# First attention with one small PE unit a step, engines' parts set apart, and experts begun from six batches

## The reference, cut to what matters

```python
x = x + attn0(layernorm(x))     # differential attention
x = x + ffn0(layernorm(x))      # 8 experts, 2 of them per token, capacity 1280 rows
x = x + attn1(layernorm(x))     # causal attention, 16 heads of 64
x = x + ffn1(layernorm(x))      # 8 experts, 4 per token, and a shared one

def attn0(x):                   # 16 heads of 8
    q, k, v = heads(x @ Wq.T + bq), heads(x @ Wk.T + bk), heads(x @ Wv.T + bv)
    x1 = softmax(q[:, :8] @ k[:, :8].T * 8 ** -0.5) @ v[:, :8]
    x2 = softmax(q[:, 8:] @ k[:, 8:].T * 8 ** -0.5) @ v[:, 8:]
    return concatenate([x1 - lv * x2, x2]) @ Wp.T + bp

def ffn0(x):
    probs, selected = top_k(softmax(x @ router.T), 2)       # probs divided by their sum
    # of each expert's tokens the 1280 with the largest weight are kept, ties in order of token
    # kept rows are dispatched to their expert's list, the rest is dropped
    out = (pre(rows) * silu(gate(rows))) @ post             # 128 -> 512 -> 128
    return sum of a token's kept outputs by its kept weights, divided by their sum
```

## Time and profile before

| | us |
|---|---|
| median of 3 runs | 1673.18 (1672.67 to 1674.95) |
| profiled execution | 1670.91 |
| its span on the core | 1667.8 |
| PE busy | 1540.4 |
| DVE busy | 1119.1 |
| ACT busy | 962.3 |
| POOL busy | 749.1 |

### The profile page before, as it was taken

How to read it: one execution, slowest core, us unless ns; L and a number is a source line. 1 busy time by engine, 2 the same in 40 slices (tenths; PEclk the granted TensorE clock), 3 DMA queues, 4 the chain that set the end, 5 groups by cost and what they waited for, 6 DMA issues and landing times.

```text
span 1667.8 us, 27765 instructions
## 1 busy us (share of the span) xinstructions
PE 1540.4 (92%) x9447; PEld 939.3 (56%) x9447; DVE 1119.1 (67%) x3559; ACT 962.3 (58%) x2484; POOL 749.1 (45%) x1237
## 2 busy tenths in 40 slices
PE   3779999998898999998899999999999999999998
PEld 2324334433334878897456565555656565657776
DVE  5669999899883567654666767767676767673322
ACT  2467767677675323333566767667675757674333
POOL 6122543453336665546453545545363634342221
PEclk9989999999999999999999999999999999999999
DMA  5447634663514565567000000000000000000000
GB/s 127 125 67 133 122 110 74 124 137 104 87 41 157 162 206 173 177 208 239 21 14 1 11 4 8 8 4 11 1 14 1 14 1 1 1 1 1 20 14 20
DMA packets 65984, 114.52 MB, mean 69 GB/s; under 512 B 13114, under 2 KB 32444, under 8 KB 65836
## 3 DMA queue, kind: packets, MB, share of 16 engines
q0 software_dynamic: 28608, 71.28, 19.3%
q1 hardware_dynamic: 36800, 40.69, 7.5%
q10 hardware_dynamic: 436, 0.79, 0.1%
HBM read 73.05 MB, written 39.78 MB: 68 GB/s over the span
## 4 chain that ended last, share of the span: by engine, by line
PE 53%; DVE 21%; ACT 11%; POOL 6%; issue 5%; DMA 4%; ACTq 0%; POOLq 0%; DVEq 0%
DVE mx L1565 7%; PE bank L1183 6%; ACT ar L1401 5%; PE pS L1150 5%; PE bank L1163 4%; PE bank L1192 4%; PE bank L992 3%; PE pS L962 3%; PE pS L1068 3%; PE pS L1069 3%; PE bank L1245 3%; PE bank L1120 3%; PE bank L1135 2%; PE bank L1083 2%; PE bank L1131 2%
## 5 line engine op out<-in xcount | busy, mean ns | idle before, releaser
L2130 POOL TENSOR_SCALAR ar<-ar,rd 128x512 f32<-128x512 f32 (+3 forms) x512 | 263.8, 535 | 305.4 <-DVE rd L1864 305.1
L1401 ACT ACTIVATE ar<-ar,nm 128x512 f32<-128x512 f32 (+3 forms) x512 | 284.9, 558 | 170.9 <-DVE nm L1855 170.7
L1565 DVE TENSOR_REDUCE mx<-pS 128x1 f32<-128x512 f32 x512 | 320.1, 680 | 54.2 <-PE pS L962 53.1
L1318 ACT ACTIVATE ar<-bank 128x512 f32<-128x512 f32 x342 | 193.9, 596 | 92.8 <-PE bank L983 92.0
L1855 DVE CUSTOM_DVE_ANT_0 ar<-pS,maskf 128x512 f32<-128x512 f32 (+3 forms) x512 | 228.2, 483 | 16.5 <-PE pS L1150 14.4
L962 PE MATMUL pS<-all_r 64*128 64x512 f32 x512 | 211.4, 493 | 27.0 <-DVE mx L1565 19.0
L1163 PE MATMUL bank<-identr,all_r 128*128 128x128 f32 x1280 | 201.0, 287 | 17.0 <-ACT ar L1411 9.5
L1163 PEld LDWEIGHTS bank<-identr,all_r 128*128 128x128 f32 x1280 | 133.0, 142 | 118.8 <-issue 81.9
L962 PEld LDWEIGHTS pS<-all_r 64*128 64x128 f32 x512 | 92.0, 198 | 174.3 <-DVE mx L1565 163.1
L1150 PE MATMUL pS<-ar 64*128 64x512 f32 (+3 forms) x1024 | 173.7, 458 | 0.0
L1357 ACT ACTIVATE ar<-pS 128x256 f32<-128x256 f32 (+1 forms) x200 | 70.3, 351 | 161.1 <-PE pS L1069 160.0
(11 more groups left out here) (251 smaller groups left out, 2858.7 us busy)
## 6 DMA issues: line engine op xcount, KB each, us to landing
rows_in<-zrow SPq DMA_DIRECT2D x16, 1024.0 KB, 4.6
all_r<-dk POOLq DMA_DIRECT2D x28, 256.0 KB, 8.4
dk<-xT SPq DMA_DIRECT2D x21, 256.0 KB, 4.4
rows_out<-ar SPq DMA_DIRECT2D x35, 128.0 KB, 4.0
dq<-xT SPq DMA_DIRECT2D x16, 256.0 KB, 2.9
all_r<-dq POOLq DMA_DIRECT2D x14, 288.0 KB, 6.6
all_r<-dq POOLq DMA_DIRECT2D x14, 256.0 KB, 4.8
x<-in_x SPq DMA_DIRECT2D x8, 256.0 KB, 3.8
```

The costliest lines, as they stand in the source:

```text
L1318: S.activation(pt[n % NPT], bST[n % 3], ACT.Exp, scale=QK_SCALE).then_inc(*s_ex.inc(Gr, kb, j))
L1401: S.activation(p, p, ACT.Exp, bias=nm1[:, c:c + 1], scale=-1.0, accum_out=den1[:, c:c + 1]).then_inc(*s_e1.inc(u, a))
L1565: V.tensor_reduce(mx[Gr % 2][:, col:col + 1], bS[n % 3], AX.X, ALU.max, negate=True).then_inc(*s_mx.inc(Gr, c))
L2130: G.tensor_scalar(p, p, rd1[:, c + a:c + a + 1], 1.0, ALU.mult, ALU.mult).then_inc(*s_p1.inc(u, a))
```

## The change

**The first attention's list.** Two functions take the generators' place. `beside(b, at)` names the one misc-bank unit of step `at` (0 to 15 within a batch), which now stands right behind the four pv and ahead of the fourth score unit. `behind(b, at)` names what the engines other than PE do at the end of the step, mostly two steps before it is used.

```diff
+    def beside(b, at):
+        Gr, p = 4 * b + at // 4, b - 1
+        if at % 4 == 0:
+            return [("shift", Gr + 1)] if Gr + 1 < NG else []
+        if at % 4 == 1:
+            return [("fin", Gr - 1)] if Gr else []
+        units = {2: ("at", p), 3: ("op", p), 6: ("v", b + 1), 7: ("turn", b + 2), 10: ("rturn", p),
+                 11: ("logits", "r", p), 14: ("q", b + 2), 15: ("k", b + 2)}
+        if b == NB - 1 and at == 6:
+            return [("table", 0)]
...
+    def behind(b, at):
+        Gr, p, n = 4 * b + at // 4, b - 1, b + 2
+        if at % 4 == 1 and Gr + 1 < NG:
+            add("land", Gr + 1)
+        if at % 4 == 3 and Gr + 2 < NG:
+            add("parts", Gr + 2)
...
                 if n == 3:
-                    if 4 * g + kb in PREP_AT:
-                        next(work, None)
                     if before[0] >= 0:
-                        for i in JS:
+                        for i in order_of(before[0]):
                             add("pv", *before, i)
+                    if kb == 0 and Gr > 0:
+                        add("take", Gr - 1)
+                    for unit in beside(b, 4 * g + kb):
+                        add(*unit)
```

**Normalization on ACT.** For batches 2 to 7 before the attention and 0 to 6 before the router:

```diff
+        def scale(stage, b, half):
+            rstd, nm = ln_sets[LN_SET[stage]][3:5]
+            ACTE.wait_ge(*s_rstd.at(stage, b))
...
+            for t in (2 * half, 2 * half + 1):
+                ins = S.activation(dst[:, t, :], x[:, 4 * b + t, :], ACT.Identity, bias=nm[:, t:t + 1],
+                                   scale=rstd[:, t:t + 1])
```

**Shift.** One transposition of 128 x 32 in place of four of 128 x 8:

```diff
-            for q in range(4):
-                ins = M.transpose(misc[0:8, 128 * q:128 * q + 128], mp[i][:, q, :], identf[:, :])
-            ins.then_inc(*s_full.inc("shift", Gr))
+            M.transpose(misc[0:32, 0:128].bitcast(F32R), mp[i][:, :, :].rearrange("p q c -> p (q c)").bitcast(F32R),
+                        identr[:, :]).then_inc(*s_full.inc("shift", Gr))
...
-            S.copy(mT[i], misc[0:8, :]).then_inc(*s_mact.inc("shift", Gr))
+            S.copy(mT[i], misc[0:32, 0:128]).then_inc(*s_mact.inc("shift", Gr))
...
-    dm = [dram(f"dm{i}", [8, 512]) for i in range(2)]
+    dm = [dram(f"dm{i}", [32, 128]) for i in range(2)]
```

```diff
+    for n, more in enumerate(([("k", 1)], [("low", "k", 1)], [("v", 1), ("zero", 1)], [])):
+        for unit in quarter(0, n) + more:
             add(*unit)
     add("parts", 0)
     add("shift", 0)
     add("land", 0)
...
+            if Gr == 0 and kb == 1:
+                add("late", 0)
+            if Gr == 2 and kb == 1:
+                add("late", 1)
```

```diff
+EARLY = 6 * 4 - (E - 1)
+PARTS = ((0, 0, EARLY), (0, EARLY, NCH[0] - EARLY), (1, 0, NCH[1]))
...
-    side = chained(last_batch(), route(NB - 1), table(1), qk_weights(), capacity())
+    side = in_turn(chained(last_batch(), route(NB - 1), table(2), qk_weights(), capacity()),
+                   chained(list_rows(NB - 2), table(1)))
```

More of the change, by code:

```diff
@@ L168, in route, with list_rows, table @@
             yield
-    def table(h):
-        add("table", h)
+            yield
+    def list_rows(b):
+        add("place", b)
         yield
-    def lead():
-        for p in range(2):
-            add("weights", p)
-            add("rows", p)
-            yield
+        yield
+        add("rows_at", b)
+        yield
+        yield
+        for t in range(4):
+            add("scatter", b, t)
+            yield
+            yield
+    def table(part):
+        add("table", part)
+        yield
@@ new lines, in in_turn @@
+    def in_turn(*parts):
+        parts = list(parts)
+        while parts:
+            for p in list(parts):
+                if next(p, p) is p:
+                    parts.remove(p)
+                else:
+                    yield
+    def beside(b, at):
[8 more added lines that the diff above has]
+            return [("table", 0)]
+        u = units.get(at)
+        return [u] if u and 0 <= u[-1] < NB and u != ("v", 1) else []
@@ L180, in schedule @@
     add("zero", 0)
-    first, second, stacks = prep(0), prep(1), stack(0)
-    for part in (first, first, second, first, second, first, first, second):
-        next(part)
+    for unit in (("ln", "p", 0), ("ones_of_v",), ("apply", "p", 0), ("ln", "p", 1), ("turn", 0), ("apply", "p", 1),
+                 ("q", 0), ("low", "q", 0), ("k", 0), ("low", "k", 0), ("turn", 1)):
+        add(*unit)
     for m in range(8):
-        next(stacks)
-    next(first)
-    for x in second:
-        pass
-    add("lam")
@@ L201, in schedule, with order_of @@
     add("land", 0)
-    for kb in range(2):
-        for unit in quarter(1, kb):
-            add(*unit)
-    PREP_AT = (9, 11, 12, 13, 14, 1)
-    STACK_AT = (0, 1, 2, 2, 3, 3, 4, 5)
-    work, proj, rout = iter(()), iter(()), []
-    ready = False
-    def route_step():
-        while rout:
-            if next(rout[0], 0) != 0:
-                return
-            rout.pop(0)
+    for b in range(2):
+        add("bias_x", b)
+    add("ones", 1)
+    for n in range(4):
+        for unit in quarter(1, n):
+            add(*unit)
+    add("lam")
+    add("parts", 1)
+    def order_of(Gr):
+        return JS if Gr + 2 < NG else (0, 1, 2, 3)
     for Gr in range(NG):
@@ L1698, in table @@
             after()
[L1699 to L1700 removed]
+            V.scalar_tensor_tensor(tiles(ridx[h][:, per * first:per * (first + nch)]), each(t_e), float(LIST[h]), loc,
+                                   ALU.mult, ALU.add).then_inc(*s_tab.inc(part))
         def hidden(p, f):
```

398 lines of the change are left out of this document (228 added, 170 removed).

## The result

The changed kernel took 1688.66 us, median of four runs (1683.43 to 1689.90), against 1672.93 before: ratio 1.0091, 95% interval 1.0063 to 1.0118. Slower, where 28 us faster was forecast. Run again later on another chip it stood at 1.0020 (0.9990 to 1.0049).

The account below looks back on a forecast made before the run. A first-attention batch was taken as DVE's work plus 5.2 us of its idle time, with PE setting the pace in the last groups. Terms -11 - 7 - 7 - 5 - 1 + 3.3 = -27.7 gave 1645 us; range 1614 to 1676.

Parts of the forecast that it names:

- Part a: Prologue to group 0's take: earlier first scores and exp, fewer maxima left for later; -11 us, bounds -2 and -16.
- Part f: Experts: earlier rows and spread scatters save, table 1 and the flush block before pass 37 cost; +3.3 us, bounds -7 and +8.
- Part c: Batches 1 to 5: normalizations leave DVE, its idle time stays; 55.0 us a batch in place of 56.4, -7 us.
- Rival B: First attention: the unit behind pv adds its whole length to DVE's hole; +50 us, 1695 us; chance 0.14.
- Part b: Groups 1 to 3: split x loads free the landing's DMA queue; 39 us in place of 45.9, -7, bounds 0 and -9.
- Part d: Batch 6: less DVE work and waiting, 51.7 us in place of 56.4; -5 us, bounds 0 and -7.
- Part e: Batch 7: table 0 moves to step 6 into DVE's slack, place goes; -1 us, bounds +2 and -4.
- Rival C: Groups 0 and 1: the new wait for x[2] keeps PE at its lower clock; 1655 us; chance 0.12.

Follow-up runs that it names:

- second pair: The changed kernel and the kernel before, both unaltered, run and profiled again on another chip: ratio 1.0020 (0.9990 to 1.0049).
- e5: Changed kernel with all stacks drawn first at each step's end, ahead of land and parts: 0.9922 of the kernel before.
- e13: Changed kernel with only the small unit moved behind the step's last score and exp product, stacks still behind parts: 1.0001 of the kernel before.
- e6: Changed kernel with stacks first and the small unit behind the step's last score and exp product: 0.9799 of the kernel before.
- e9: Changed kernel with stacks first, unit last, table 0 at step 14 of batch 7, weights and rows 0 and 1 behind it: 0.9825 of the kernel before.
- e11: Changed kernel with stacks first, unit last, table 0 at step 8 of batch 7: 1648.30 us, 0.9859 of the kernel before; 0.9796 on another chip.
- e15: Changed kernel with stacks first, unit last, table 0 at step 8, last two groups' exp and pv in old order 0, 2, 1, 3: 0.9794 of the kernel before.
- e10: Changed kernel with stacks first, unit last, table 0 at step 14 of batch 7, shift in its old form: 0.9787 of the kernel before.
- e1: Changed kernel with only the eighth stack moved, to the end of step 4, ahead of land: 1675.47 us, 1.0036 of the kernel before.
- e3: Changed kernel with table 0 at step 7 of batch 7 in place of step 6: 1.0062 of the kernel before.
- e2: Changed kernel with the shift in its old form (four transpositions, 8 pieces of 2 KB), order untouched: 1678.07 us, 1.0036 of the kernel before.

## Why the prediction was wrong, by its steps

- **Part a was right in sum**: -10.9 against -11, take 0 at 78.03 against 78, and it is -11.3 in the second pair. Its terms were off both ways: the first scores start at 32.2 us (31 forecast) and the first exp at 60.2 (58.3 forecast, so 3.0 us won and not 4.9), while from there to take 0 it is 7.9 us less where 5.8 was forecast. The stretched normalization was read rightly: it takes 1.12 us now.
- **Part f** was right in sum in the first pair, +3.8 against +3.3, and in kind: 12.7 us at the flush are 9 more than the neighbours, and the first pass no longer waits for rows. That the sum fits is partly luck. From the last take to the first transposition it gave -1.6 (forecast -2.5), from there to the last outward product +2.9 (forecast +5.8), and behind that, where nothing was forecast, +2.4, which no run explains. In the second pair f is +11.3, +8.1 of it between the first transposition and the last outward product.
- **Part c is the step that failed.** The work was right (48.95 us of DVE against 48.9, ACT's normalization 0.48 us against 0.46, ACT's 42 us no bound). The idle time was not: I wrote 5.3 us and "0.7 for the k rows that land from DRAM"; it was 11 in batch 4 and 9.2 to 11.5 in batches 1 to 5. Two things are in it. First, POOL's queue: PE waits 14.0 us for dk in six batches, 2.3 a batch, and mending it won 2.2 us a batch alone (e5) and 3.1 with the unit moved (e13 to e6). I had listed what `behind` does and seen that stacks kept their steps, but not that inside a step they had changed places with parts. The shift's way I "cost at nothing, since the landing is used two steps on": true of the exp that it feeds, untrue of what stands behind land in POOL's queue.
- Second, "some 0.35 us more that its queued work does not cover" at five units a batch: the hole is 0.73 us behind q and 0.68 behind k, and only the unit's place makes it; with both orders mended the same units left 2.2 us of wait for scores in a whole batch. There a batch's idle time is 53.56 - 48.84 = 4.7 us, near my 5.3: the estimate fitted an order that the change did not have.
- **Rival B** named this mechanism, with its place, but priced it at the unit's whole length, 8.4 us a batch; the unit's place measured 2.2 (alone) to 3.1 us, 13 to 19 us in six batches. B alone would not have eaten the gain of 28. It took the queue, which was in no rival, and batch 7.
- **Part b** gave -2.3 of -7: group 1 still took 17.6 us. The split of the x loads did not free it; PE waited there 1.3 us for the landing and 2.6 us for dk.
- **Part d** gave +0.2 of -5: DVE's idle time was 9.7 us in place of 6.0, by the same two causes, and its work 47.0 in place of 45.8. With both orders mended batch 6 takes 51.7 us (e6), the length forecast.
- **Part e**: +9.3 against -1. I wrote that table 0 goes "into DVE's slack"; but at step 6 DVE has none, scores still come, and PE waited 4.75 us. Its slack begins at step 8. That wait accounts for half; the rest is PE at its 1.2 GHz level in the steps without scores, 24 us of batch 7 against 10 before. The low clock stood there for 10 to 43 us in every profile of the new list but e9's, wherever the table was, and for 29 us in the second profile of the kernel before, whose batch 7 took 59.4 us. Neither the table's place (e11) nor the last groups' order (e15) removed it. Its cause stays open.
- **Rival C** (the clock) was put into groups 0 and 1. That place lost nothing of note, score matmuls first came to 0.39 to 0.50 us at 75 us, where it had been 80 us before; the clock cost time where C had no term. The Trainium skill ("TensorE: Matmul & The Clock Gate", section "HAM oscillation — how this bites in real kernels") has waits between bursts throttle the engine again. The changed kernel's batch 7 fits that in part: its first low stretch begins in the 4.75 us wait. e9 and e10, one list but for the shift's form, PE's longest wait 1.4 us in both and 47.5 against 61.1 us, show that the same waits don't always bring it.

Put together: with stacks first and the unit last, batches 1 to 5 take 269.2 us in e6, part c at -12.6 against the first profile of the kernel before in place of +14.1, where -7 was forecast.

## What to carry to other kernels

When an order is rewritten, compare each in-order queue entry by entry inside a step too, the DMA queues first: a load that keeps its step but falls behind an operation that waits is late, and takes with it all that is behind. Keep a matmul engine's unrelated pieces apart from each other by the work that feeds its slowest consumer, at most as much between two feeds as the full buffers cover (here 1.86 us). And when one late item is moved, look what stands next in that queue before believing in the gain: e1 moved one stack and batches 2 to 5 stayed at 58 to 60 us, e5 moved all eight and they came to 56.7 in the mean.

## What the hardware showed that was not expected

- One program's PE clock differs more between two profiled executions, here of two chips, than most edits are worth: 34 and 72 us at 1.2 GHz from 80 to 540 us of the same kernel before, whose batches took 55.6 to 57.8 us in one and 55.2 to 61.2 in the other.
- DMA pieces of 512 bytes in place of 2 KB slowed the shift's way little, by some 0.6 us at step 4 (e3 against e2). The loads issued just ahead weigh more: from the shift's DMA to land it is 4.1 to 5.2 us behind one load issued 3.8 us ahead (kernel before), 7.2 to 8.6 behind three within 2 us (changed kernel) and 8.7 to 9.4 behind four (e1).
- In-order queues hide their price: the same wait of land, 5.14 us in the changed kernel and 4.14 in e5, goes with 14.0 us of PE's waits for dk in six batches or with none, by what is queued behind it.
